# Token lists of six experts built in DRAM by indirect transfers instead of by one-hot matmuls

## The reference

```python
    x = x + _L0_xattn_ref(_layernorm(x, axis=-1), ctx_768, L0_xattn_Wq, L0_xattn_Wk, L0_xattn_Wv, L0_xattn_Wo, L0_xattn_bo)
    x = x + _L0_ffn_ref(_layernorm(x, axis=-1), L0_ffn_gate_w, L0_ffn_w1, L0_ffn_w2)
...
        k = int(EXPERT_CAPACITY * t / e)
        scores = jnp.einsum('ntd,ed->nte', x, gate_w)
        probs = jax.nn.softmax(scores, axis=-1)
        g, m = jax.lax.top_k(probs.transpose(0, 2, 1), k)
        batch_idx = jnp.arange(n)[:, None, None]
        xin = x[batch_idx, m]
        h = jnp.einsum('nekd,edf->nekf', xin, w1)
        h = jax.nn.gelu(h, approximate=False)
        h = jnp.einsum('nekf,efd->nekd', h, w2)
        out_tok = g[..., None] * h
        out = jnp.zeros((n, t, d), dtype=x.dtype).at[batch_idx, m].add(out_tok)
```

## Time and profile before

| | |
|---|---|
| median of three runs | 1688.56 us (1688.48 to 1689.51) |
| the profiled execution, its own time | 1689.17 us |
| its span in the trace | 1687.5 us |
| granted TensorE clock, mean | 0.998 |
| PE busy | 1667.5 us, 99% of the span |
| PEld busy | 1426.7 us, 85% |
| DVE busy | 1088.0 us, 64% |
| ACT busy | 828.7 us, 49% |
| POOL busy | 347.6 us, 21% |
| packets of the software queue q0 (GpSimd's) | 14336, 33.56 MB |

### The profile page before, as it was taken

The page is one execution under the profiler, slowest core; times in us unless marked ns, Lnnn a source line. Parts: engine busy times, 40 slices in busy tenths (PEclk is TensorE's granted clock), DMA queues, the critical chain, the costliest instruction groups (busy, mean ns, idle before and its releaser), DMA issues.

```text
span 1687.5 us, 23422 instructions
## 1 busy us (share of the span) xinstructions
PE 1667.5 (99%) x8714; PEld 1426.7 (85%) x8714; DVE 1088.0 (64%) x2004; ACT 828.7 (49%) x1931; POOL 347.6 (21%) x412
## 2 busy tenths in 40 slices
PE   8999999999999999999999999999999999999997
PEld 8999999877888888888888888888888888888886
DVE  6555797877766657655755575557555755675663
ACT  5678777633333334444544464445444544464441
POOL 3233234111121023300240034003400430041002
PEclk9999999999999999999999999999999999999999
DMA  3242435334334252511341134113411341142003
GB/s 132 76 147 103 150 129 216 126 118 125 125 87 170 70 149 102 148 50 50 76 125 51 50 76 125 50 50 78 122 50 50 84 116 50 50 88 63 25 1 50
DMA packets 76678, 156.40 MB, mean 93 GB/s; under 512 B 4461, under 2 KB 5641, under 8 KB 76569
## 3 DMA queue, kind: packets, MB, share of 16 engines
q1 hardware_dynamic: 62201, 121.36, 21.1%
q0 software_dynamic: 14336, 33.56, 10.0%
q10 hardware_dynamic: 32, 0.03, 0.0%
HBM read 121.38 MB, written 33.55 MB: 92 GB/s over the span
## 4 chain that ended last, share of the span: by engine, by line
PE 97%; DVE 1%; ACT 1%; DMA 0%; issue 0%; POOL 0%; POOLq 0%; SPq 0%; DVEq 0%
PE ps L2061 10%; PE ps L2060 10%; PE ps L2062 10%; PE ps L2038 9%; PE ps L2039 9%; PE ps L2040 9%; PE ps L1219 4%; PE ps L1221 4%; PE ps L1220 4%; PE ps L1953 4%; PE ps L1954 3%; PE ps L1955 3%; PE ps L1940 3%; PE ps L1942 3%; PE ps L1941 3%; PE ps L1997 1%
## 5 line engine op out<-in xcount | busy, mean ns | idle before, releaser
L2060 PE MATMUL ps<-v2h,hhS 128*128 128x512 f32 x768 | 300.5, 391 | 0.0
L2062 PE MATMUL ps<-v2h,hlS 128*128 128x512 f32 x768 | 298.9, 389 | 0.0
L2061 PE MATMUL ps<-v2l,hhS 128*128 128x512 f32 x768 | 298.9, 389 | 0.0
L2038 PE MATMUL ps<-Th,Wh 128*128 128x512 f32 x672 | 261.4, 389 | 0.0
L2039 PE MATMUL ps<-Tl,Wh 128*128 128x512 f32 x672 | 261.4, 389 | 0.0
L2040 PE MATMUL ps<-Th,Wl 128*128 128x512 f32 x672 | 261.4, 389 | 0.0
L1502 POOL DMA_INDIRECT out_dram<-YS,tok_idx x48 | 83.0, 1729 | 804.9 <-DVE YS L1862 796.5
L1648 ACT ACTIVATE v2h<-w_raw 128x512 fp32r<-128x512 f32 x96 | 57.5, 623 | 308.7 <-PE ps L2062 308.7
L1862 DVE SCALAR_TENSOR_TENSOR YS<-ps,tok_gate,YS 128x512 f32<-128x512 f32 x144 | 106.6, 749 | 132.2 <-PE ps L2062 132.2
L2062 PEld LDWEIGHTS ps<-v2h,hlS 128*128 128x128 f32 x768 | 144.1, 188 | 30.1
L2060 PEld LDWEIGHTS ps<-v2h,hhS 128*128 128x128 f32 x768 | 144.2, 188 | 29.4
(11 more groups left out here) (279 smaller groups left out, 3588.2 us busy)
## 6 DMA issues: line engine op xcount, KB each, us to landing
w_raw<-in_L_ffn_w_dram SPq DMA_DIRECT2D x80, 1024.0 KB, 5.6
XB<-in_x_dram SPq DMA_DIRECT2D x16, 512.0 KB, 4.2
XR<-in_x_dram SPq DMA_DIRECT2D x16, 512.0 KB, 6.3
out_dram<-X SPq DMA_DIRECT2D x16, 512.0 KB, 5.2
xn_rows<-XN SPq DMA_DIRECT2D x16, 512.0 KB, 5.5
w_raw<-in_L_xattn_Wq_dram SPq DMA_DIRECT2D x1, 1024.0 KB, 8.6
wo_sb<-in_L_xattn_Wo_dram SPq DMA_DIRECT2D x2, 512.0 KB, 11.1
w_raw<-in_L_xattn_Wk_dram SPq DMA_DIRECT2D x1, 768.0 KB, 5.1
```

The lines of the kernel that those rows point to most:

```text
L2038: nc.tensor.matmul(ps[:, bank, :], wh, th, start=(idx in OPENS and k == 0), stop=False, **go_on)
L2060: nc.tensor.matmul(ps[:, bank, :], th, wh, start=(t == 0), stop=False)
L2061: nc.tensor.matmul(ps[:, bank, :], th, wl, start=False, stop=False)
L2062: last = nc.tensor.matmul(ps[:, bank, :], tl, wh, start=False, stop=(t == GF - 1))
```

## The change

Experts 0 and 1 keep their lookups. For the twelve columns of experts 2 to 7 the list goes through DRAM. GpSimd fills `pairs` with each token's number (`iota`), VectorE its probability (`dve_pairs`), and `dve_list_places` computes for each token where in the column's list it goes: its place, or a place of its own beyond 512 if it isn't chosen. For each column and each of 16 tiles of 128 tokens one indirect transfer writes 128 pairs of 8 bytes to `lists` (`write_lists`, 192 transfers of 128 rows). When all have landed, each column's first 512 entries are read back with one plain transfer (`read_lists`, 12 transfers), and gathers, scatters and `evict` use `tok_pair` in place of `tok_idx` and `tok_gate`. The 192 transfers are put between the gathers and scatters of the plain columns by hand.

```diff
--- before
+++ after
@@ -42,2 +42,3 @@
     xn2_rows = nc.dram_tensor("xn2_rows", (B * S, D), F32, kind="Internal").ap()
+    lists = [nc.dram_tensor(f"list{c}", (CAP + S, 2), U32, kind="Internal").ap() for c in range(COLS)]
     x_blk = x.rearrange("b (n t p) d -> (b n) p t d", t=TPB, p=P)
@@ -179,3 +180,3 @@
         c_const = sem("c_const")
-        CONSTS = 16
+        CONSTS = 17
         c_vx = sem("c_vx")
@@ -279,2 +280,4 @@
                       allow_small_or_imprecise_dtypes=True).then_inc(c_const, 1)
+            pool.iota(away[:], pattern=[[P, NT]], base=CAP, channel_multiplier=1,
+                      allow_small_or_imprecise_dtypes=True).then_inc(c_const, 1)
             pool.wait_ge(c_const, CONSTS)
@@ -505,3 +508,8 @@
         PR = put("PR", 163840, [P, TPB, H, J])
+        NPE = 2
         nmax = fixed("nmax", [P, TPB, H])
+        away = fixed("away", [P, NT])
+        tok_pair = fixed("tok_pair", [P, COLS, CT, 2], U32)
+        list_at = fixed("list_at", [P, B, E - NPE, NT], U32)
+        pairs = put("pairs", 59392, [P, B, E - NPE, NT, 2], U32)
         ssum = fixed("ssum", [P, TPB * H])
@@ -725,4 +733,18 @@
 
+        def dve_list_places(dve, b):
+
+            shape = [P, E - NPE, NT]
+            far = away[:].unsqueeze(1).broadcast_to(shape)
+            link(nc.vector.tensor_tensor(q1[:, NPE:E], place[:, NPE:E], far, ALU.subtract))
+            link(nc.vector.tensor_tensor(q2[:, NPE:E], q1[:, NPE:E], chosen[:, NPE:E], ALU.mult))
+            nc.vector.tensor_tensor(list_at[:, b], q2[:, NPE:E], far, ALU.add).then_inc(v_list, 1)
+
+        def dve_pairs(dve, b):
+
+            nc.vector.tensor_copy(pairs[:, b, :, :, 1].bitcast(F32), probs[:, b, NPE:E, :]).then_inc(v_pairs, 1)
+
         def dve_rows(dve, b):
 
+            dve_list_places(dve, b)
+            dve.wait_ge(v_list, b + 1)
             link(nc.vector.tensor_scalar(q1[:], place[:], float(P), None, ALU.is_ge))
@@ -794,4 +816,6 @@
         PLAIN = (0, 1, E, E + 1)
-        NPE = len(PLAIN) // B
-        LOOKUPS = PLAIN + tuple(b * E + e for e in range(NPE, E) for b in range(B))
+        LOOKUPS = PLAIN
+        d_list, d_tok, v_list, v_pairs, g_pairs = (sem(n) for n in "d_list d_tok v_list v_pairs g_pairs".split())
+
+        LISTS = tuple((b, x) for b in range(B) for x in range(E - NPE))
 
@@ -1183,3 +1207,3 @@
                 if at(i, CHOICE + 2):
-                    dve_vals(0, 1, E // 2)
+                    dve_vals(0, 1, NPE)
                 if at(i, 0):
@@ -1482,5 +1506,23 @@
 
+            def write_lists(first, last):
+                for m in range(first, last):
+                    b, x = LISTS[m]
+                    if x == 0:
+                        pool.wait_ge(v_list, b + 1)
+                        pool.wait_ge(v_pairs, b + 1)
+                        pool.wait_ge(g_pairs, B)
+                    for t in range(NT):
+                        pool.indirect_dma_start(out=lists[b * E + NPE + x],
+                                                out_offset=bass.IndirectOffsetOnAxis(ap=list_at[:, b, x, t:t + 1], axis=0),
+                                                in_=pairs[:, b, x, t, :], in_offset=None).then_inc(d_list, 16)
+
+            def read_lists(x):
+                pool.wait_ge(d_list, 16 * NT * len(LISTS))
+                for b in range(B):
+                    c = b * E + NPE + x
+                    pool.dma_start(tok_pair[:, c], lists[c][0:CAP, :].rearrange("(p q) v -> p q v", p=P)).then_inc(d_tok, 16)
+
             def gather_pair(x, b):
                 c = b * E + NPE + x
-                pool.wait_ge(h_idx, LOOKUPS.index(c) + 1)
+                pool.wait_ge(d_tok, 16 * B * (1 if x == 0 else NS))
                 if x:
@@ -1491,3 +1533,3 @@
                     pool.indirect_dma_start(out=rows_in[b][:, q, :], out_offset=None, in_=xn2_rows,
-                                            in_offset=bass.IndirectOffsetOnAxis(ap=tok_idx[:, c, q:q + 1], axis=0),
+                                            in_offset=bass.IndirectOffsetOnAxis(ap=tok_pair[:, c, q, 0:1], axis=0),
                                             ).then_inc(s_rows, 16)
@@ -1502,3 +1544,3 @@
                 pool.indirect_dma_start(out=out_rows,
-                                        out_offset=bass.IndirectOffsetOnAxis(ap=tok_idx[:, c, q:q + 1], axis=0),
+                                        out_offset=bass.IndirectOffsetOnAxis(ap=tok_pair[:, c, q, 0:1], axis=0),
                                         in_=YS[:, j, :], in_offset=None, compute_op=ALU.add,
@@ -1517,8 +1559,22 @@
                 pool.wait_ge(d_x1[u], 16 * NBLK // 2)
-            for i in range(len(PLAIN) - 1):
-                pool_gather(pool, i + 1)
-                if i == len(PLAIN) - 2:
-                    gather_pair(0, 1)
-                scatter(i)
+            for b in range(B):
+                pool.iota(pairs[:, b, :, :, 0], pattern=[[0, E - NPE], [P, NT]], base=b * S,
+                          channel_multiplier=1).then_inc(g_pairs, 1)
+            write_lists(0, 1)
+            pool_gather(pool, 1)
+            write_lists(1, 4)
+            scatter(0)
+            write_lists(4, 6)
+            pool_gather(pool, 2)
+            write_lists(6, 8)
+            scatter(1)
+            write_lists(8, 9)
+            pool_gather(pool, 3)
+            write_lists(9, 12)
+            read_lists(0)
+            gather_pair(0, 1)
+            scatter(2)
             gather_pair(0, 0)
+            for x in range(1, NS):
+                read_lists(x)
             t_low(0, 0)
@@ -1602,2 +1658,3 @@
                 if n == T_AT[3] + 1:
+                    act.wait_ge(d_list, 16 * NT * len(LISTS))
                     for idx in W_ORDER[0:3]:
@@ -1749,4 +1806,4 @@
                     dve_one_hot(hot_of[n])
-                if n == 2:
-                    dve_vals(0, E // 2, E)
+                if n == 0:
+                    dve_pairs(dve, 0)
                 if n == 3:
@@ -1765,3 +1822,4 @@
                 if n == VALS_AT:
-                    dve_vals(1, 0, E)
+                    dve_vals(1, 0, NPE)
+                    dve_pairs(dve, 1)
                 if n == T_AT[3]:
@@ -1849,3 +1907,3 @@
                 x, g = divmod(n, G)
-                gate = tok_gate[:, j // CT * E + NPE + x, j % CT:j % CT + 1]
+                gate = tok_pair[:, j // CT * E + NPE + x, j % CT, 1:2].bitcast(F32)
                 src = ps[:, D_BANKS[j % 3], :]
@@ -1857,2 +1915,3 @@
                         dve.wait_ge(f_scat, 16 * CT * len(PLAIN))
+                        dve.wait_ge(d_tok, 16 * B * NS)
                     nc.vector.tensor_scalar(YS[:, j], src, gate, None, ALU.mult).then_inc(s_ev, 1)
```

## The result

The changed kernel takes **1717.1 us** (median of 4 runs, 1715.2 to 1719.7) where the kernel before took 1688.7 on the same chip: ratio 1.0164, 95% interval 1.0152 to 1.0177, so 28 us slower. The forecast was 1700 us. The sign was right, the size was not: +28 instead of +11. The profiled execution took 1717.15 us with a span of 1715.2.

A forecast was written before the change was run, and what follows sets the result against it. TensorE was taken to bound the kernel, with GpSimd last at the pair after the change. Terms of -6.0 + 2.9 + 1.7 + 12.4 = +11.0 us turned 1689.2 into 1700 us; own range 1692 to 1712, wide range 1682 to 1720.

The forecast's parts named there:

- What goes on TensorE: Twelve lookups of 0.50 us each go from TensorE, all before the pair's first transpose at 621.81 us: 6.0 us less.
- VectorE: Twelve one-hots and most `vals` go, small operations come; VectorE isn't in the chain there: counted 0, at most 0.5 us to win.
- What bounds it: TensorE, 97% of the last chain, bounds the kernel before; once GpSimd is last at the pair, its date replaces TensorE's.
- The floor of a write: Price of one GpSimd list write, taken from the gather: 1.26 us start to start, with bounds 0.67 and 1.89 kept.
- 192 x 1.26 = 242 us: GpSimd's list writes at the gather's pitch, to fit into less than 300 us beside gathers and scatters.
- the rival that gave 1718: VectorE's casts hold up GpSimd's list writes: 42 casts each add 0.43 us, 18 us on top; chance 0.09.
- reads, to the gather of batch 1: Two plain list reads on GpSimd, the second issued 1.26 us behind the first at 603.8, landed at 607.6.
- scatter 2, gather of batch 0, landing: GpSimd's last piece before the pair's first transpose takes what it took before, 20.2 us, ending at 632.8.
- steady whatever VectorE does: A GpSimd gather's 0.95 us doesn't depend on VectorE; used against the writes being cheaper than gathers.
- Dearer writes: Writes cost like the summing scatter (1821 us), or the DMA engines set the pace (1746 us); chance 0.08.
- Landing: The last list write lands 3.8 us after issue, as the gather does; weight loads on the shared DMA engines counted 0.
- The dates: TensorE's gathered rows at columns 1, 2, 3 and the pair: in time, then 2.9, 1.7 and 12.4 us late.

The follow-up runs named there:

- experiment 1: Kernel before, without its 12 lookups for the six experts: pairs take indices and gates of experts 0 and 1, no lists; 1683.33 us, ratio 0.9965.
- experiment 5: Changed kernel with gathers 2 and 3 and scatters 0 and 1 one list of 16 writes further ahead, that list written after gather 3; 1722.58 us.
- experiment 3: Changed kernel with weight loads from the third group on cut to a 128 x 128 corner; 1716.14 us, ratio 1.0155.
- experiment 4: Changed kernel with w1l, w2l and hl made by one-input operations and weight loads from the third group on cut to a corner; 1703.55 us, ratio 1.0082.
- experiment 2: Changed kernel with VectorE's w1l and w2l made by a one-input operation in place of the two-input subtraction; 1711.57 us, ratio 1.0124.

## Why the prediction was right and wrong

**Right.** *What goes on TensorE*: 6.0 us forecast, 5.6 measured (experiment 1). *VectorE*: counted as 0; rows 9 reads 2.1 before and after. *What bounds it*: once GpSimd is last, its date replaces TensorE's. That was the rule of the sum, and experiment 5 shows it: TensorE's waits can be moved from the columns to the pair, and the time follows the pair's date. *The floor of a write*: 0.96 + 0.30 = 1.26 us was taken from the gather, and the median write in the trace takes 0.959.

**Wrong: "192 x 1.26 = 242 us".** The term was mis-sized: a floor was used as a mean. The 192 writes took 1.048 + 0.30 = 1.35 us each, 17 us more than forecast, and that is the size of the miss (I had named a pitch off by more than 0.05 as what would make it wrong; it is off by 0.09). That the rest of the sum comes out even is luck: landing and reads were off by +5.1 and -2.5 us, the piece behind them by -4.7. The forecast's own range, 1692 to 1712, missed the result; the wide one, 1682 to 1720, held it only because it also took in the rival that gave 1718. By the sum's own steps, forecast against measured:

| step | forecast | measured | difference |
|---|---|---|---|
| last write ends, with its gap | 600.0 | 617.0 | +17.0 |
| from there to the reads | 2.5 | 7.6 | +5.1 |
| reads, to the gather of batch 1 | 5.1 | 2.6 | -2.5 |
| that gather | 5.0 | 5.5 | +0.5 |
| scatter 2, gather of batch 0, landing | 20.2 | 15.5 | -4.7 |
| pair's first transpose | 632.8 | 648.2 | +15.4 |
| from there to the end of the span | 865.7 | 867.0 | +1.3 |

The fifth row is the same mistake the other way round. The 20.2 us were taken from before as one piece, and that piece held a gather that a one-hot had prolonged to 2.95 us (598.84) and a landing of 6.0 us; after the change they took 0.95 and 4.1 (the third and the fourth transfer).

**What I should have read.** The excess was in the trace of before. I had seen gathers of 1.14 and 1.39 us, put them down to VectorE's casts as a rival, and then ruled VectorE out by rows 11 ("steady whatever VectorE does"). Two views of before, at one instant that I didn't look at, GpSimd's and VectorE's:

```profile
505.57 2.94 POOL L908 DMA_INDIRECT XB<-xn_rows,tok_idx  x1 [0.30 <-issue]
```

```profile
505.40 2.28 DVE L767 TENSOR_TENSOR hot<-row,col_iota 128x2048 bf16<-128x2048 f32 x1
```

0.95 + (505.40 + 2.28 - 505.57 - 0.13) = 2.93. The same sum gives 1.40 for the gather of 344.23, under the `w2l` of 344.12, and it took 1.39. Rows 11 were no counterexample: that cast began 0.33 us after the gather, and an operation that begins later doesn't hold the gather up, as the `hl` of 384.14 doesn't. The rule on copies of the Trainium skill (SBUF — State Buffer, section "SBUF: two separate sides"), which I weighed and set aside, holds here for casts that begin first: five writes began behind one, with 0.4 us of excess. The rest is in "Who interferes with whom" (the Trainium skill, SBUF — State Buffer): a VectorE instruction with two inputs in SBUF contends with a GpSimd instruction that reads SBUF, one with a single input and outside the two-port modes doesn't, and issue order decides who blocks. The trace agrees on the first two (`w2l` as subtraction and as one-input operation). On the third it agrees for GpSimd alone: of 28 `hl` that began over 0.13 us into a write none took more than 0.694 us, no longer than with no write beside them. And where the section infers that such a two-input instruction leaves the making of descriptors alone, the runs differ: under one, 455.50 took 2.49 us.

**The rival that gave 1718** was "VectorE's casts hold up the writes" with a chance of 0.09. It gave nearly the right time, by luck: its reason holds for 0.4 us of the 17.0. Casts do hold a write up, but only when they started first, and there were five such meetings, not 42: the casts last 0.43 us and the wait begins to count 0.13 us after the write's start. The two-input operations make nearly all the rest. *Dearer writes*: the DMA engines were no limit; q0's share grew from 10.0 to 10.8%.

**Landing.** 3.8 us was taken from gather 1, and it was the least of the five that the trace of before has for the last transfers of the gathers between 325 and 622 us. The one of gather 2, issued at 451.69 (line 908, a view of before):

```profile
DMA to landing us min/median/max: 7.0/7.0/7.0
```

The reads waited 9.1 us from the last write's start. With next to no weight data in the queues it is 5.4 and 7.0 (experiments 3 and 4). With all of it, but other dates, it was 10.1 and 6.6 in experiments 2 and 5. So the weight load issued at 611.65 and 612.06 has a part in the 9.1, where I had counted 0. A window of the changed kernel shows it (stretch, its length, busy us and instructions of each engine, granted clock, DMA share, GB/s):

```profile
615.00:621.00 6.00, 6.00 (x28) 4.97 (x27) 2.94 (x6) 1.95 (x4) 1.39 (x2) 1.00 0.92 343
```

By the trace's packet records the last list write ended on GpSimd at 616.69, but its last packet was moved at 621.1, among the weights' packets. With the weight loads cut (experiment 3) the same distance is 0.8 us instead of 4.4, and that is the 3.6 us. What remains is common to the runs: from the last list packet to the read it is 3.5 us here and 2.7 to 4.4 in experiments 2 to 5, while a gather has landed at most 0.9 us after its last packet. Why, is open.

**The dates.** Forecast waits of 0, 2.9, 1.7 and 12.4 us at columns 1, 2, 3 and the pair came as 2.8, 15.0, 2.3 and 9.7. Column 2's is the largest miss: its last transfer was issued 12.2 us later than in the sum (475.92 against 463.7) and landed after 6.1 us instead of 3.8. By experiment 5 it cost nothing: it only spends early what the pair would wait for.

**The clock.** The last 1.3 us of the table come from TensorE's clock after it has stood. Windows of the changed kernel (stretch, its length, busy us and instructions of each engine, granted clock, DMA share, GB/s):

```profile
640.00:648.00 8.00, 0.00 (x0) 0.00 (x0) 0.00 (x0) 0.00 (x0) 6.88 (x10) 0.62 0.98 251
648.00:652.00 4.00, 3.80 (x13) 3.41 (x14) 0.00 (x0) 0.00 (x0) 2.45 (x5) 0.50 0.10 7
652.00:660.00 8.00, 8.00 (x36) 6.55 (x36) 3.51 (x6) 3.35 (x7) 0.00 (x0) 0.99 0.00 0
```

TensorE has no matmul from 640 to 648, the granted clock falls, and the first matmuls behind the wait run at 0.50, the level of 1.2 GHz; by 652 to 660 it is back at 2.4. The 16th matmul behind the pair's first transpose starts 4.60 us after it where it was 2.73 before, 1.9 us later, and the 1000th is still 1.9 us later; 0.6 us of it is made up by the end. I had no term for this.

## What to carry to other kernels

Before work is put on GpSimd's indirect transfers, set the trace's own transfers beside VectorE's rows of the same instants: the price is a floor plus what is left of the VectorE operation under which each one starts, where that is a cast or has both inputs in SBUF, and the mean, not the floor, has to be multiplied. When a queue has a last consumer, its place in the order is worth more than its price: the same 192 writes cost 34 us or nearly nothing, by whether the first reader waits for 32 of them or for all. And a stall ahead of a later, fixed date is no loss by itself; add up dates, not waits.

## What the runs showed that I had not expected

- An indirect transfer's instruction on GpSimd that starts while VectorE runs an operation with two inputs in SBUF, or a float32 cast, with more than 0.13 us of it left, ends 0.83 us after that operation (0.96 - 0.13); 455.50 took 2.49 us. With the same operation made one-input, 43 meetings cost 0.1 us in all, and with one input in PSUM six cost nothing. An operation that starts a little later than the transfer costs it nothing, unless it follows at once on one that the transfer is waiting for: the write of 439.75 had a `w1l` beside it and then the `w2l` of 439.86, and took 1.62 us. Where both start within 0.04 us, the write can get off free and VectorE pays: five `hl` that began 0.04 us ahead of a write took 0.77 us instead of 0.69, and the writes 0.96.
- A list write's 128 rows of 8 bytes don't make the 8 packets for each engine that I had counted: 192 writes and 12 reads added 6528 packets in all for 24576 rows. By the packet records a write is 16 packets of 64 bytes and 16 of 4 bytes. The 3072 packets of 64 bytes took 62 us of the 16 engines together, 0.02 us each, where one of before took 0.19 on the average.
- The last list write became readable 5.4 to 10.1 us after its start; the last transfer of a gather landed after 3.8 to 7.3 us before the change and 4.1 to 7.1 after it.
